# Sliding-window attention: 128-row matmul tiles against 64x64 tiles, with the band added on TensorE

## The reference

```python
nb = s // W                                   # W = 64, 16 heads of 16
q, k, v = ((x @ Wx + bx).reshape(b, nb, W, H, HD) for x's three weights)
kc, vc = blocks n-1, n, n+1 of k and v, side by side        # 192 keys a block of 64 queries
scores = einsum('bnqhd,bnkhd->bhnqk', q, kc) / sqrt(HD)
mask = (abs(i + W - j) <= W) & key exists     # i in 0..63, j in 0..191
attn = softmax(where(mask, scores, -1e9))
out = einsum('bhnqk,bnkhd->bnqhd', attn, vc) @ Wo + bo
...                                           # residual, layer norm, W1, gelu, W2, layer norm,
...                                           # top-1 of 8 experts (a 256x256 product), residual
```

## Time and profile before

| what | us |
|---|---|
| three runs | 1558.44, 1560.16, 1561.64 |
| median | 1560.16 |
| span of the profiled execution | 1553.1 |
| median less span | 7.1 |
| PE busy | 1240.9 (80%) |
| DVE busy | 1071.5 (69%) |
| ACT busy | 739.8 (48%) |
| POOL busy | 739.9 (48%) |

### The profile page before, as it was taken

The page is one execution under the profiler, slowest core; times in us unless marked ns, Lnnn a source line. Parts: engine busy times, 40 slices in busy tenths (PEclk is TensorE's granted clock), DMA queues, the critical chain, the costliest instruction groups (busy, mean ns, idle before and its releaser), DMA issues.

```text
span 1553.1 us, 34323 instructions
## 1 busy us (share of the span) xinstructions
PE 1240.9 (80%) x10696; PEld 714.8 (46%) x10696; DVE 1071.5 (69%) x3743; ACT 739.8 (48%) x1356; POOL 739.9 (48%) x749
## 2 busy tenths in 40 slices
PE   0648885999678985999859997689858898599967
PEld 0424452735346353654527454373535535265435
DVE  8656775777757775867757677576766676587565
ACT  1305744366543744447443565426544374445642
POOL 6443745156531766037550474406752177504661
PEclk9959997999989997989979899798988899799979
DMA  7463056220733119130462206422082212912010
GB/s 237 92 139 118 3 117 122 76 92 29 144 79 100 57 69 166 50 112 13 108 131 69 99 8 145 91 83 83 33 156 75 88 57 74 162 48 94 2 28 28
DMA packets 89647, 135.00 MB, mean 87 GB/s; under 512 B 10209, under 2 KB 62305, under 8 KB 87393
## 3 DMA queue, kind: packets, MB, share of 16 engines
q1 hardware_dynamic: 83328, 115.91, 30.0%
q0 software_dynamic: 6144, 16.79, 4.4%
HBM read 74.47 MB, written 59.90 MB: 87 GB/s over the span
## 4 chain that ended last, share of the span: by engine, by line
PE 49%; DMA 17%; issue 11%; POOL 8%; DVE 8%; SPq 3%; ACT 3%; DVEq 0%; POOLq 0%; ACTq 0%
DMA pair_dram<-pool 9%; PE bank L1132 8%; PE bank L1035 8%; PE bank L1154 8%; PE bank L1036 7%; PE bank L1038 7%; PE bank L1181 6%; DMA q_s<-q_s 5%; DVE xn L604 2%; SPq L284 2%; DMA ys_dram<-xn 2%; PE bank L1102 2%; POOL x_sb L453 2%; POOL x_sb L451 2%; POOL rs L386 2%
## 5 line engine op out<-in xcount | busy, mean ns | idle before, releaser
L713 DVE CUSTOM_DVE_ANT_0 bank<-bank,mask 128x192 f32<-128x192 f32 x1024 | 337.3, 388 | 199.1 <-PE bank L1132 195.1
L943 ACT ACTIVATE pool<-bank 128x512 f32<-128x512 f32 x512 | 293.0, 597 | 118.9 <-PE bank L1154 113.2
L1132 PE MATMUL bank<-k_s,q_s 128*64 128x192 f16 x2048 | 175.3, 269 | 144.1 <-DMA q_s<-q_s 141.2
L440 POOL TENSOR_SCALAR_AFFINE_SELECT pool<-pool 128x512 f32<-128x512 f32 x256 | 172.2, 675 | 194.1 <-ACT pool L943 193.4
L1154 PE MATMUL bank<-q_s,k_s 128*128 128x256 f16 x1024 | 199.3, 290 | 28.7 <-issue 21.3
L389 POOL TENSOR_TENSOR rs<-ve,neghalf 128x1 f32<-128x1 f32 x64 | 36.9, 577 | 384.8 <-DVE ve L776 384.8
L1132 PEld LDWEIGHTS bank<-k_s,q_s 128*64 128x64 f16 x2048 | 77.8, 113 | 250.1 <-issue 226.9
L1181 PE MATMUL bank<-pool,v_a 128*32 128x256 f32 (+2 forms) x2560 | 161.1, 345 | 19.9 <-DVE pool L727 8.6
L989 ACT ACTIVATE pool<-bank,c1c 128x512 f32<-128x512 f32 x128 | 87.8, 686 | 169.5 <-PE bank L1038 132.5
L790 DVE TENSOR_TENSOR pool<-pool 128x512 f16<-128x512 f32 x128 | 106.7, 839 | 63.3 <-ACT pool L955 62.2
L713 DVE DVE_READ_ACCUMULATOR2_ANT m_sb<- 128x1 f32 x1024 | 144.6, 141 | 0.3
(11 more groups left out here) (149 smaller groups left out, 2511.1 us busy)
## 6 DMA issues: line engine op xcount, KB each, us to landing
pair_dram<-pool SPq DMA_DIRECT2D x32, 512.0 KB, 7.6
xn<-xs_dram SPq DMA_DIRECT2D x40, 384.0 KB, 3.7
ys_dram<-xn SPq DMA_DIRECT2D x120, 128.0 KB, 1.7
q_s<-pair_dram SPq DMA_DIRECT2D x48, 256.0 KB
k_s<-pair_dram SPq DMA_DIRECT2D x48, 256.0 KB
x_sb<-in_L_attn_x SPq DMA_DIRECT2D x8, 1024.0 KB, 5.7
res_dram<-x_sb SPq DMA_DIRECT2D x8, 1024.0 KB, 4.8
res_r<-res_dram SPq DMA_DIRECT2D x8, 1024.0 KB, 7.4
```

The costliest lines, as they stand in the source:

```text
L440: nc.gpsimd.affine_select(out=p, in_=p, compare_op=ALU.is_ge, fill=0.0, base=0, pattern=[[0, 4], [1, 2 * W]], channel_multiplier=-1).then_ ...
L713: ins = nc.vector.tensor_tensor_reduce(out=SB[u % 2][:, i * WIN:i * WIN + WIN], in0=SB[u % 2][:, i * WIN:i * WIN + WIN], in1=mask[:, v, :] ...
L943: nc.scalar.activation(prob[:, (k + 2) % 3, 2 * pu:2 * pu + 2, :], TB[u % 2][:, :].rearrange("p (h q) -> p h q", h=2), ACT.Exp, scale=EXP_ ...
L1132: mm = nc.tensor.matmul(SB[u % 2][W * bl:W * bl + W, i * WIN:i * WIN + WIN], q_s[:, h, W + w0:2 * W + w0], k_s[:, h // 2, w0:w0 + WIN], st ...
```

## The change

Both score products become matmuls on 64x64 tiles of the array. Row half (partitions 0 to 63 or 64 to 127) is the parity `par` of the head, column half is the block n of 64 queries or keys in the tile. So q_s keeps one slice for a pair of heads (its size halves), and nothing needs a zeroed other half. The first product contracts only the KW = 48 rows of the slots, so the row of the maxima may hold anything, and the two copies inside q_s go. The second product makes 192 queries for a key block where it made 256 for a tile. A call of scores_t(k, par) now interleaves its matmuls one by one with those of scores(k+13, 1-par), 4 and 4, and then adds the band to both with 4 matmuls of an identity (bf16) by a mask of 2 x 2 x 64 columns; DVE's and POOL's masks go. The maxima are two plain tensor_reduce of 128 x 384 a step. The exponentials are 128 x 384. The values are split by key block: blocks in the lower partitions add up in banks 4 and 5, those in the upper ones in banks 6 and 7, in 64x32 tiles; ACT copies the first pair, and DVE adds the second to it (heads_sum). With banks 6 and 7 taken, the maxima's transposes share banks 0 and 1 with the scores. A list MAX_STEPS says which scores must wait until DVE has read a transpose. Each wait on PE in these functions is followed by `sem_inc(passed, 1)`.

```diff
     STEPS = G * T
-    SHARED = range(22, 28)
-    QW = 4 * W
+    KW = 3 * HD
+    MAX_STEPS = [LEAD - T + 3] + [T * g + MAX_AT - 1 + LEAD for g in range(G - 2)]
-        mask = sb("mask", [P, 3, WIN], BF16)
+        ident16 = sb("ident16", [P, W], BF16)
+        mask = sb("mask", [P, 3, 2, W], BF16)
-        q_s = sb("q_s", [P, H, S + 2 * W], F16)
+        q_s = sb("q_s", [P, H // 2, S + 2 * W], F16)
-        SB, TB, OB, MB = bank[0:2], bank[2:4], bank[4:6], bank[6:8]
+        SB, TB, OB = bank[0:2], bank[2:4], bank[4:6]
+        MB = SB
+        PV = (bank[4:6], bank[6:8])
-        NSTACK = 2 * 2 * 3 + 2
+        NSTACK = 2 * 2 * 3
...
-                for a in range(2):
-                    r = W * a + 3 * HD
-                    sp.dma_start(q_s[r:r + 1, a:H:2, W:W + S], q_s[r:r + 1, 1 - a:H:2, W:W + S]).then_inc(stack.sem, 16)
...
-            def band(b, k):                      # POOL, its two affine_selects
...
             def turn(b, last):                   # POOL
-                for k in range(STEPS):
-                    band(b, k)
-                    if k == XN_AT - 1 and not last:
-                        rstd(b + 1, 0, ve0, rs0)
                 if not last:
+                    rstd(b + 1, 0, ve0, rs0)
                     residual(b + 1)
...
             def maxima(b, j):                    # DVE
-                    for i in range(2):
-                        ins = nc.vector.tensor_tensor_reduce(
-                            out=SB[u % 2][:, i * WIN:i * WIN + WIN], in0=SB[u % 2][:, i * WIN:i * WIN + WIN], in1=mask[:, v, :], scale=1.0,
-                            scalar=-3.0e38, op0=ALU.add, op1=ALU.max, accum_out=m_sb[:, h, t:t + 1])
+                    nc.vector.tensor_reduce(m_sb[:, 4 * g + par:4 * g + 4:2, t],
+                                            SB[par][:, 0:2 * WIN].rearrange("p (h c) -> p h c", h=2), AX.X, ALU.max).then_inc(mx.sem, 1)
+            def heads_sum(b, g, hf):
+                dve.wait_ge(oT_ev.sem, oT_ev.at(b, 2 * g + hf + 1))
+                o = oT[:, g, hf * HALF:hf * HALF + HALF]
+                nc.vector.tensor_tensor(o, PV[1][hf][:, :], o, ALU.add).then_inc(oT_sum.sem, 1)
...
+            def score_mm(out, n, j, par, i):     # PE
+                h, r = 2 * g + i, slice(W * par, W * par + KW)
+                q = W + (2 * t + n) * W
+                return nc.tensor.matmul(out[W * n:W * n + W, i * WIN:i * WIN + WIN], q_s[r, h, q:q + W], k_s[r, h, q - W:q + 2 * W],
+                                        start=i == 0, stop=False, skip_group_check=True)
+            def mask_mm(out, n, t, par):
+                band = mask[r, edge(2 * t + n), :, :].unsqueeze(1).broadcast_to([W, 2, 2, W])
+                return nc.tensor.matmul(dst, ident16[r, :], band, start=False, stop=True, skip_group_check=True)
+            def scores_wait(b, j, par, first=False):
+                if not first or u >= 2:
+                    pe.wait_ge(mx.sem, mx.at(b, u - 1))
+                    pe.sem_inc(passed, 1)
+                if j in MAX_STEPS and par == 1:
+                    pe.wait_ge(mT_ev.sem, mT_ev.at(b, MAX_STEPS.index(j) + 1))
+                    pe.sem_inc(passed, 1)
-            def max_cols(b, g):
-                pe.wait_ge(mx.sem, mx.at(b, 2 * T * (g + 1)))
+            def max_cols(b, g, issued):
+                pe.wait_ge(mx.sem, mx.at(b, 2 * issued))
             def scores_t(b, k, par):
                 if u >= 2:
                     pe.wait_ge(ex_done.sem, ex_done.at(b, u - 1))
+                    pe.sem_inc(passed, 1)
+                if both:
+                    scores_wait(b, j, 1 - par)
                 for i in range(2):
+                    for n in range(2):
+                        score_t_mm(TB[par], n, k, par, i)
+                        if both:
+                            score_mm(SB[1 - par], n, j, 1 - par, i)
+                for n in range(2):
+                    mt = mask_mm(TB[par], n, t, par)
+                    if both:
+                        ms = mask_mm(SB[1 - par], n, j % T, 1 - par)
             def values(b, k):
-                pe.wait_ge(masked.sem, masked.at(b, 2 * k + 2 - shared))
+                pe.wait_ge(ex_done.sem, ex_done.at(b, 2 * k + 2))
+                pe.sem_inc(passed, 1)
+                for hl in range(4):
+                    for a, hf, blk, lo, hi in pieces:
+                        mm = nc.tensor.matmul(PV[a][hf][32 * hl:32 * hl + 32, (lo - T * hf) * W:(hi - T * hf) * W],
+                                              v_a[r, t, 4 * g + hl, :], prob[r, (k + 2) % 3, hl, c:c + (hi - lo) * W],
                                               start=first, stop=last, skip_group_check=True)
```

More of the change, by code:

```diff
@@ L402, in _ @@
             step(nc.gpsimd.memset(q_s[:, :, :].rearrange("p h s -> p (h s)").bitcast(F32), 0.0))
-            step(nc.gpsimd.memset(mask[:, :, :], 0.0))
+            step(nc.gpsimd.memset(mask[:, :, :, :], 0.0))
             step(nc.gpsimd.memset(ones16[:, :], 1.0))
@@ L831, in turn @@
                         c1_stage(b + 1)
-                    if k in SHARED:
-                        band(b, k)
+                    if k >= LAG + 5 and (k - LAG) % T == 5:
+                        heads_sum(b, (k - LAG) // T, 0)
+                    if k > LAG and (k - LAG) % T == 0:
+                        heads_sum(b, (k - LAG) // T - 1, 1)
                     if XN_AT <= k < XN_AT + T // 2 and not last:
@@ L838, in turn @@
                         xn_low(b + 1, k - (STEPS - 4))
+                heads_sum(b, G - 1, 1)
                 b_stage(b)
@@ L1137, in max_cols @@
-            def max_cols(b, g):
-                pe.wait_ge(mx.sem, mx.at(b, 2 * T * (g + 1)))
+                    pe.sem_inc(passed, 1)
+                    if not first:
+                        pe.wait_ge(nT_l.sem, nT_l.at(b - 1, 4))
+                        pe.sem_inc(passed, 1)
[4 more added lines that the diff above has]
+                    pe.wait_ge(mT_ev.sem, mT_ev.at(b, MAX_STEPS.index(j) + 1))
+                    pe.sem_inc(passed, 1)
@@ new lines, in scores @@
+            def scores(b, j, first=False):
+                for par in (1, 0):
+                    scores_wait(b, j, par, first)
+                t = j % T
+                for i in range(2):
+                    for n in range(2):
+                        for par in (1, 0):
+                            score_mm(SB[par], n, j, par, i)
+                for n in range(2):
+                    for par in (1, 0):
+                        mm = mask_mm(SB[par], n, t, par)
+                        if n == 1:
+                            mm.then_inc(S_ps.sem, 1)
@@ new lines, in values @@
+                    pe.sem_inc(passed, 1)
+                pieces = []
+                for a in range(2):
+                    blk = 2 * t + a
+                    for hf in range(2):
+                        lo, hi = max(blk - 1, T * hf, 0), min(blk + 2, T * hf + T)
+                        if lo < hi:
+                            pieces.append((a, hf, blk, lo, hi))
+                for hl in range(4):
+                    for a, hf, blk, lo, hi in pieces:
+                        first = blk in (0, 1) if hf == 0 else blk in (T - 1, T)
+                        last = blk in (T - 1, T) if hf == 0 else blk in (2 * T - 2, 2 * T - 1)
+                        c = (lo - blk + 1) * W
+                        r = slice(W * a, W * a + W)
+                        mm = nc.tensor.matmul(PV[a][hf][32 * hl:32 * hl + 32, (lo - T * hf) * W:(hi - T * hf) * W],
+                                              v_a[r, t, 4 * g + hl, :], prob[r, (k + 2) % 3, hl, c:c + (hi - lo) * W],
@@ L1280, in turn @@
                     if k % T == MAX_AT and k < 3 * T:
-                        max_cols(b, k // T + 1)
-                    for pu in range(2):
+                        max_cols(b, k // T + 1, min(k - 1 + LEAD, STEPS))
+                    for par in range(2):
                         if k < STEPS:
-                            scores_t(b, k, pu)
-                        if 1 <= k and k - 1 + LEAD < STEPS:
-                            scores(b, k - 1 + LEAD, half=pu)
+                            scores_t(b, k, par)
                     if STEPS - 4 <= k < STEPS and not last:
```

149 lines of the change are left out of this document (62 added, 87 removed).

## The result

The changed kernel is slower: 1615.8 us, median of 4 runs (1610.7 to 1618.7), against 1559.3 before. The ratio is 1.037, 95% interval 1.034 to 1.040. The profiled execution has a span of 1617.0.

A forecast was written before the change was run, and what follows sets the result against it. PE, busy 80% of the span, was taken to bound the kernel. A turn gives 6.4 - 3.0 - 0.8 + 1.7 + 0.4 = 4.7; eight give 37.6, plus 4.9 and 3.9: 1560.2 - 46.4 = 1514 us, range 1480 to 1585.

The forecast's parts named there:

- the step's sum: Attention loop, regular step with both score products: waits (links) 0.36, call 0.47, release 0.06, exp 0.49, together 1.38 us.
- B: Attention loop: waits cost nothing because PE's sequencer runs ahead; step 1.12 us, total 1483; chance 0.12.
- C: Attention loop: tiles of different row halves don't run side by side; step 1.97 us, total 1589; chance 0.13.
- E: Attention loop: DVE takes the gain, reduce 0.78 and late links; step 1.65 us, total 1548; chance 0.07.
- F: Attention loop: weight loads don't hide, the closing loop grows by 0.14 us; total 1545; chance 0.06.
- max_cols: Loop, k = 4 and 12: PE waits for last reduce, transposes and DVE's reading, 1.5 us each; 3.0 lost a turn.
- heads_sum: Loop, on DVE four times between two reduces: 0.2 us each, 0.8 lost a turn.
- The second part: Loop's 12 steps without the second product (scores): 16.0 us against 17.8, taken as 1.7 won a turn.
- Rival D: Attention loop: with fewer columns and more pauses PE's clock falls to 1.2 GHz; step 1.97 us, total 1650; chance 0.08.
- The end of the loop: After the last exp: values no longer wait for two bands, but heads_sum precedes b_stage's transposes; 0.4 us won.
- The copies: Between loads and first scores: without the copies inside q_s, scores start 0.7 us earlier; seven turns, 4.9.
- The start: Kernel start: the halved memset of q_s holds DVE's normalization less; 3.9 us won.

The follow-up runs named there:

- e9_values_f16: The changed kernel with probabilities and v in float16, each values matmul one pass instead of two (low halves left out): 1597.9 us, ratio 1.025.
- e1_free_bank: The changed kernel with the maxima's transposes in bank 7, idle at k = 4, 12 and 20, instead of the scores' banks: 1584.3 us, ratio 1.014.
- e2_loads_later: The changed kernel with the loads of the next x and the residual moved behind the maxima's rows of groups 2 and 3: 1611.1 us, ratio 1.033.
- e3_shift_code: The changed kernel with 128 semaphore increments on PE where it waits for the copies of q and k, shifting later instructions: 1648.0 us, ratio 1.055.
- e8_free_bank_early_loads: e1_free_bank with the loads of the next x and the residual (2 MB) at the turn's start: 1578.7 us, ratio 1.014.

## Why the prediction was wrong

**What bounds the kernel, and the step's sum: right.** 1.38 forecast, 1.39 measured where nothing disturbs a step; each term (reduce, exp, call, two links) was within 0.02. The row halves run side by side. Rivals B, C, E and F are refuted by the step.

**max_cols: right in size; heads_sum: low.** The drains were priced at 28 us, and taking them away gave 32. heads_sum was priced at 0.2 each, and no run takes it away. In the last turn, which has no pause at k = 8, the steps that begin with it (k = 8 and 16) take 1.91 and 1.90 instead of 1.36: 1.1 for two of the four, where 0.8 was priced for all.

**The second part failed.** Forecast 16.0 us, measured 20.4 to 23.1 in the seven turns that prepare the next sequence, against 17.8 to 18.7 before. Its warm steps are 1.13 to 1.33, as assumed, but a pause stands at k = 23 and the clock is down for 12.5 us after it. At k = 28, where PE transposes the next x, 3.5 us stand instead of 1.6; how much of this is the clock's, no run separates. The last turn, which prepares no other, took 19.0 against 15.5, with a pause of 1.2 us at k = 28.

**The step of the prediction that failed** is the one that was not there: the sum took PE's instructions as always at hand and its clock as up after the first two steps. It could have been seen that the order grows from 45 to some 85 instructions a step while the step shrinks by more than a fifth, and that the page of the profile counts the blocks of instructions (q8) among the transfers of the same 16 DMA engines as the 2 MB. By the medians of the six turns, two pauses (2.7 and 2.0) and 20.8 us more at the lower clock, which stretches a step from 1.39 to 2.03 (20.8 x (1 - 1.39 / 2.03) = 6.6), make 11.3 us. Forecast and measurement of the loop differ by 4.3 + 7.1 = 11.4. This estimate leaves no room for heads_sum, so its closeness is partly luck. The last turn shows as much: with pauses of only 0.9 and 1.2 us and 11.5 us at the lower clock instead of none, its loop still took 52.3 us against 48.1, and these account for 5.7 of the 8.5 between forecast and measurement.

**Rival D had the right sign and half the right mechanism.** The clock does fall to 1.2 GHz, and a cold step was 2.03 (priced 1.97), but for half of the loop and not all, since pauses bring it down. Its "against", that PE streams for over half of the loop, did not hold. I gave it 0.08, for want of a thought on what could make PE pause. That pauses bring the clock down is shown; that they account for all the time at the lower level is not (in e9_values_f16 it is down in most of the loop, with one pause).

**Outside the loop.** The end of the loop gave 0.15 instead of 0.4 (the values end 1.26 earlier, the reciprocal comes 1.11 later behind them). The copies gave nothing instead of 4.9: what comes earlier is held by GpSimd's operations. The start gave 1.4 (first exp at 136.9 and 135.5) instead of 3.9, and that is one trace each: with the same start the first exp stood at 131.4 in e1_free_bank and at 136.2 in e2_loads_later. Scores in d_stage took 2.7 more a turn instead of 0; half a microsecond was priced for the drain there, and the excess is gone in e3_shift_code, where DVE isn't held.

## What to carry to other kernels

Count the instructions that the busiest engine must be fed per microsecond, beside its busy time: as means over the loop, 25 and 35 a us on PE went without pauses here, 35 had one in another kernel, and in those at 41 to 46 nearly every turn had two or more, the longer one while large loads filled the DMA engines. Look at the other engines' blocks too, since moving the loads can starve one of them. Price a pause of PE with what the clock takes after it (here 2 us and more behind pauses of over 2), and expect a gain that thins out PE's work to be partly given back by the clock. A transfer taken from the end of a chain is worth only what the next stage can use at its new time.

## What the runs showed that was not expected

Matmuls on different row halves overlap even when six of one half stand before six of the other in the program (starts 0.02 apart, steps unchanged at 1.39). A DVE operation of 0.69 us beside a GpSimd operation of 4.5 us lasted up to 5.0 us, and up to 7.6 beside several shorter ones. Idle times of PE (1.5 to 3.4 us) and of DVE (2.9 to 3.6 us, e8_free_bank_early_loads) that nothing else in the timeline explains ended 2.2 to 3.3 and 1.8 to 1.9 us behind the start of a block of instructions. A semaphore increment on PE took 0.13 us.
